# A four-layer transformer in one kernel: set-up order, first mask layout, routing in parts and block indices changed

## The reference

```python
x = x + L0_xattn(layernorm(x), ctx, mask0)     # 16 heads; mask0 is 4 x 1 x 512 x 77, bool
x = x + L0_ffn(layernorm(x))                   # 8 experts, top 2 by softmax, gelu
x = x + L1_xattn(layernorm(x), ctx, mask1)     # 16 heads; mask1 is 4 x 77, int
x = x + L1_ffn(layernorm(x))                   # sum over 8 gated experts, silu, no routing
x = x + L2_xattn(ctx, layernorm(x), mask2)     # 16 heads; mask2 is 1 x 1 x 512 x 77, bool
x = x + L2_ffn(layernorm(x))                   # 1 shared and 8 routed experts, top 2, silu
x = x + L3_xattn(ctx, layernorm(x))            # 8 heads of 128; keys are x's 512 rows and ctx's 77
x = x + L3_ffn(layernorm(x))                   # 8 gated experts, top 2, silu
```

## Time and profile before

| | us |
|---|---|
| runs | 1589.42, 1583.72, 1591.42 |
| median | 1589.42 |
| profiled execution | 1584.89 |
| its span on the core | 1581.8 |
| PE busy | 1386.6 (88%) |
| VectorE busy | 1028.4 (65%) |
| ScalarE busy | 850.9 (54%) |
| GpSimd busy | 545.0 (34%) |

### The profile page before, as it was taken

One profiled execution on the slowest core, in us unless ns is written; L12 is line 12 of the kernel. 1 busy time (PEld: TensorE's weight loads), 2 busy tenths in 40 slices (PEclk: granted clock), 3 DMA queues, 4 the chain that ended last, 5 costly groups with the idle time before them and its releaser, 6 DMA issues.

```text
span 1581.8 us, 21944 instructions
## 1 busy us (share of the span) xinstructions
PE 1386.6 (88%) x7201; PEld 1099.5 (70%) x7201; DVE 1028.4 (65%) x2075; ACT 850.9 (54%) x1608; POOL 545.0 (34%) x880
## 2 busy tenths in 40 slices
PE   3899798798999999889999997699989989875992
PEld 3565576554888888756678885588878878765992
DVE  4545678755666666845567775577777877655773
...
GB/s 153 33 92 2 61 114 94 41 80 63 193 101 99 113 88 120 103 38 61 45 50 107 54 1 1 118 42 1 1 12 5 1 16 1 36 139 117 382 249 87
DMA packets 67790, 123.13 MB, mean 78 GB/s; under 512 B 10200, under 2 KB 43792, under 8 KB 66399
## 3 DMA queue, kind: packets, MB, share of 16 engines
...
...
## 4 chain that ended last, share of the span: by engine, by line
PE 67%; DVE 12%; POOL 10%; issue 7%; ACT 2%; DMA 2%; ACTq 0%; POOLq 0%; DVEq 0%; SPq 0%
PE psum L2003 11%; PE psum L2005 11%; PE psum L2004 11%; PE psum L2248 5%; PE psum L2388 4%; PE psum L2390 4%; PE psum L2389 4%; PE psum L2483 3%; PE psum L2201 2%; PE psum L2202 2%; POOL y_dram L994 2%; POOL slots_dram L963 2%; DMA shared<-in_mask_dram 1%; PE psum L2028 1%; PE psum L2232 1%
## 5 line engine op out<-in xcount | busy, mean ns | idle before, releaser
L1816 DVE TENSOR_TENSOR hhl<-psum,hhl 128x512 fp32r<-128x512 f32 x336 | 230.2, 686 | 83.6 <-ACT hhl L1282 81.5
L1282 ACT ACTIVATE hhl<-psum 128x512 fp32r<-128x512 f32 x336 | 199.3, 593 | 3.4 <-DVE psum L1812 3.2
L2003 PE MATMUL psum<-xh,wl 128*128 128x512 f32 x464 | 189.2, 408 | 3.2 <-DVE hhl L1816 2.5
L2004 PE MATMUL psum<-xl,wh 128*128 128x512 f32 x464 | 184.7, 398 | 0.0
L2005 PE MATMUL psum<-xh,wh 128*128 128x512 f32 x464 | 184.4, 397 | 0.0
L1062 POOL TENSOR_SCALAR shared<-shared,xstat 128x589 f32<-128x589 f32 x128 | 97.7, 765 | 232.4 <-DVE xstat L1906 231.9
L1272 ACT ACTIVATE psum<-psum 128x512 f32<-128x512 f32 x208 | 120.9, 582 | 71.3 <-PE psum L2005 70.0
L1354 ACT ACTIVATE hhl<-psum 128x512 fp32r<-128x512 f32 (+1 forms) x160 | 95.4, 596 | 116.9 <-PE psum L2483 116.6
L2388 PE MATMUL psum<-hhl,wl 128*128 128x512 f32 x336 | 135.0, 402 | 12.8 <-DVE xn L1836 9.4
L1812 DVE TENSOR_TENSOR psum<-act_out,psum 128x512 f32<-128x512 f32 x128 | 89.0, 696 | 84.0 <-PE psum L2005 78.5
L1911 DVE TENSOR_TENSOR hhl<-psum,hhl 128x512 fp32r<-128x512 f32 (+1 forms) x160 | 110.3, 689 | 49.6 <-ACT hhl L1354 49.0
...
## 6 DMA issues: line engine op xcount, KB each, us to landing
...
```

The costliest lines, as they stand in the source:

```text
L1282: a.activation(hh[k % 4], h_bank(f, k), ACT.Copy).then_inc(f.hh_done, 1)
L1816: v.tensor_tensor(hl[k % 4], h_bank(f, k), hh[k % 4].bitcast(f32), ALU.subtract).then_inc(f.h_ready, 1)
L2003: mm(dst, ll, rh, start=start, stop=False)
L2004: mm(dst, lh, rl, start=False, stop=False)
```

## The change

It has six parts.

1. SyncE loads the first batch's x ahead of all else, with a semaphore of its own (`first_loaded`); ScalarE loads the other three batches. VectorE makes the first statistics on that semaphore.
2. The masks of layers 0 and 2 are loaded with four consecutive tokens to a partition (308 bytes in one piece), and `copy_mask` writes them in an order that undoes this. The tiles of masks 1 and 2 lie elsewhere in `shared`.
3. `keys_values(2)`, `first_stats(3)`, `masks` and `gates_split` leave VectorE's set-up for slots 1, 3, 11 and 14 of the first attention, and ScalarE's `keys_high(2)` for slot 0; the column products go from slot 13 to slot 17. The gates are counted on `mask_done`.
4. `rank_routes` is cut in `logits_in`, `compare_routes` and `order_routes`. In the attentions and feed-forward loops the last of them moves one slot later, to the weighing. In the wide loop `logits_in` and `place_rows` move one slot earlier, ahead of the low half of the turned tile, `order_routes` one later, and ScalarE's exponent one later.
5. `mask_keys` of the next layer comes once behind each of the first four splits in the loop instead of four times ahead of them.
6. `block_meta` makes the index with one operation from a destination that already has the offset in it; `valid`, `away` and what is needed for them go from `block_tables`, and rows past an expert's count carry no offset and so fall out of range by themselves.

```diff
-                    13: ("cols", 0), 15: ("x", 3)}, LEFT, LEFT]
+                    17: ("cols", 0), 15: ("x", 3)}, LEFT, LEFT]
...
         def _(sp):
+            sp.dma_start(x[:, tiles(0), :], x_in[0].rearrange("(t p) d -> p t d", p=P)).then_inc(first_loaded, 16)
             sp.dma_start(ctxT[:], ctx_t).then_inc(ctx_loaded, 16)
...
-            sp.dma_start(m2u, mask2.rearrange("b o (t p) k -> p (b o t) k", p=P)).then_inc(late_loaded, 16)
+            sp.dma_start(m2u, mask2.rearrange("b o (p t) k -> p (b o t) k", p=P)).then_inc(late_loaded, 16)
...
-                    sp.wait_ge(tables, 2)
-                at = sp.value_load(tab[0:1, 1, j - NSTAT:j - NSTAT + 1], min_val=0, max_val=NE * CAP - BK)
+                    sp.wait_ge(tables, 1)
+                at = sp.value_load(tab[0:1, 1, j - NSTAT:j - NSTAT + 1], min_val=0, max_val=NE * CAP)
...
                 pool.wait_ge(row_in[j % len(row_in)], row_landed(j))
-                w = wid[j % 4]
+                w, fields = wid[j % 4], rowin[j % RIN][:, :, D:RW].rearrange("p c (w e) -> p c w e", w=2)
                 if j < NSTAT:
-                    fields = rowin[j % RIN][:, :, D:RW].rearrange("p c (w e) -> p c w e", w=2)
-                    if j == 0:
-                        pool.wait_ge(tables, 1)
                     st.link(g.tensor_copy(w, fields[:, :, :, j]))
                 else:
                     if j == NSTAT:
-                        pool.wait_ge(tables, 2)
-                    fields = rowin[j % RIN][:, :, D:RW].rearrange("p c (w e) -> p c w e", w=2)
+                        pool.wait_ge(tables, 1)
                     st.link(g.tensor_tensor(picked, fields, bcast(bcast(dyn[:, j - NSTAT, :], 2, 1), 2, 1), ALU.mult))
                     for n in (4, 2):
                         st.link(g.tensor_tensor(picked[:, :, :, 0:n], picked[:, :, :, 0:n], picked[:, :, :, n:2 * n],
                                                 ALU.add))
                     st.link(g.tensor_tensor(w, picked[:, :, :, 0], picked[:, :, :, 1], ALU.add))
-                st.link(g.tensor_tensor(idf, w[:, :, 1], valid[:, j, :], ALU.mult))
-                st.link(g.tensor_tensor(idf, idf, away[:, j, :], ALU.add))
                 if j >= 4:
                     pool.wait_ge(y_sent[(j - 4) % 3], results_sent((j - 4) // 3 + 1))
-                g.tensor_copy(idx[j % 4], idf).then_inc(meta_ready, 1)
+                g.tensor_scalar(idx[j % 4], w[:, :, 1], FAR, 0.0, ALU.add, ALU.add).then_inc(meta_ready, 1)
...
                     pool.wait_ge(k3_in[l + 1], 16 * 12)
                     pool.wait_ge(t_ready, UL * (l + 1))
-                    for b in range(B):
-                        mask_keys(l + 1, b)
                 for e in range(f.U, f.E):
                     split(f, e)
+                    if l < 2 and e - f.U < B:
+                        mask_keys(l + 1, e - f.U)
                     if f is F1:
...
-                a.activation(maskT[:, mask_slot(l, b), :], src[0:KC, :], ACT.Copy).then_inc(mask_in, 1)
+                a.activation(maskT[:, mask_slot(l, b), :].rearrange("k (p t) -> k t p", t=TB),
+                             src[0:KC, :].rearrange("k (t p) -> k t p", t=TB), ACT.Copy).then_inc(mask_in, 1)
...
-            a.dma_start(x[:], x_in.rearrange("b (t p) d -> p (b t) d", p=P)).then_inc(x_loaded, 16)
-            a.dma_start(m0u, mask0.rearrange("b o (t p) k -> p (b o t) k", p=P)).then_inc(mask_loaded, 16)
+            a.dma_start(x[:, TB:NT, :], x_in[1:B].rearrange("b (t p) d -> p (b t) d", p=P)).then_inc(x_loaded, 16)
+            a.dma_start(m0u.rearrange("p (b t) k -> p b (t k)", b=B),
+                        mask0.rearrange("b o (p t) k -> p (b o) (t k)", p=P)).then_inc(mask_loaded, 16)
...
-            keys_high(2)
...
                     elif u == 0 and l == 0:
-                        act.wait_ge(mask_done, 2)
+                        act.wait_ge(mask_done, 1)
...
+                    if l == 0 and n == 0:
+                        keys_high(2)
...
                             x_turned(b)
-                    for what, b in WPLAN.get(n - 2, []):
+                    for what, b in WPLAN.get(n - 3, []):
                         if what == "l":
                             route_exp(F3, b)
...
-            def rank_routes(f, b, src):
+            def logits_in(f, b, src):
...
-                order_routes(f, b)
-
-            def order_routes(f, b):
+
+            def compare_routes(f, b):
...
                 st.link(v.tensor_tensor(tied, other, mine, ALU.is_equal))
                 st.link(v.tensor_tensor(tied, tied, bcast(tri[:], TB, 1), ALU.mult))
+
+            def order_routes(f, b):
+                c = tiles(b)
+                lg = logits[:, c, :]
+                mine, other = bcast(lg, NE, 3), bcast(lg, NE, 2)
                 st.link(v.tensor_tensor(above, other, mine, ALU.is_gt))
                 st.link(v.tensor_tensor(above, above, tied, ALU.add))
...
-                st.link(v.tensor_copy(rem[:, 0:NSTAT], cnt))
-
-                def validity(j):
-                    n = j.stop - j.start
-                    st.link(v.tensor_tensor(valid[:, j, :], bcast(cols2, n, 1), bcast(rem[:, j], 2, 2), ALU.is_lt))
-                    return v.tensor_scalar(away[:, j, :], valid[:, j, :], -FAR, FAR, ALU.mult, ALU.add)
-
-                validity(slice(0, NSTAT)).then_inc(tables, 1)
...
-                st.link(v.tensor_tensor(pick, dyn, bcast(cnt, NDYN, 1), ALU.mult))
-                st.link(v.tensor_reduce(blk_n, pick, AX.X, ALU.add))
-                st.link(v.tensor_tensor(rem[:, NSTAT:NBLK], blk_n, blk_i, ALU.subtract))
                 st.link(v.tensor_tensor(blk_r, blk_r, blk_i, ALU.add))
                 st.link(v.tensor_scalar(tab[:, 0, :], blk_e, float(NE - 1), None, ALU.min))
-                st.link(v.tensor_scalar(tab[:, 1, :], blk_r, float(NE * CAP - BK), None, ALU.min))
-                validity(slice(NSTAT, NBLK)).then_inc(tables, 1)
+                v.tensor_scalar(tab[:, 1, :], blk_r, float(NE * CAP), None, ALU.min).then_inc(tables, 1)
...
-                v.tensor_scalar(betaB[:], betaB[:], pcols[:, 5:6], None, ALU.mult).then_inc(gate_done, 1)
+                v.tensor_scalar(betaB[:], betaB[:], pcols[:, 5:6], None, ALU.mult).then_inc(mask_done, 1)
...
+            dve.wait_ge(first_loaded, 16)
+            first_stats(0)
             dve.wait_ge(x_loaded, 16)
-            first_stats(0)
...
-            keys_values(2)
-            masks()
-            first_stats(2)
-            first_stats(3)
-            gates_split()
             wide_weights_low(0, 0, bank(3))
             wide_weights_low(0, 1, bank(7))
+            first_stats(2)
+
+            def beside_scores(n):
+                if n == 1:
+                    keys_values(2)
+                elif n == 3:
+                    first_stats(3)
+                elif n == 11:
+                    masks()
+                elif n == 14:
+                    gates_split()
...
+                    if l == 0:
+                        beside_scores(n)
...
-                            rank_routes(f, b, bank(6))
+                            logits_in(f, b, bank(6))
+                            compare_routes(f, b)
...
+                            order_routes(f, b)
...
+                    for what, b in WPLAN.get(n, []):
+                        if what == "l":
+                            logits_in(F3, b, bank(7))
+                        elif what == "c":
+                            place_rows(b)
                     if n >= TURN:
                         turned_low(n - TURN)
                     for what, b in WPLAN.get(n - 1, []):
                         if what == "l":
-                            rank_routes(F3, b, bank(7))
-                        elif what == "c":
-                            place_rows(b)
+                            compare_routes(F3, b)
+                    for what, b in WPLAN.get(n - 2, []):
+                        if what == "l":
+                            order_routes(F3, b)
...
-                pe.wait_ge(gate_done, 1)
+                pe.wait_ge(mask_done, 3)
```

30 lines of the change are left out of this document (14 added, 16 removed).

## The result

| | before | after |
|---|---|---|
| median of 7 runs, us | 1584.76 | 1569.22 |
| lowest to highest | 1583.58 to 1591.42 | 1566.58 to 1576.07 |
| profiled execution: span, us | 1581.8 | 1565.0 |

The ratio is 0.9906, 95% interval 0.9883 to 0.9930: 15.5 us less, where 22.9 were forecast. The changed kernel is faster by more than 0.5%, and its time lies in the stated range.

What follows compares the result with a forecast made beforehand. TensorE work or waits were taken to bound the first attention, with 39.4 us touchable overall. Terms -14.7 + 4.8 + 5.8 - 4.5 - 1.3 - 9.5 - 3.5 = -22.9 gave 1562.0 profiled, 1566.5 us median; range 1553 to 1580.

Steps and rivals of the forecast that it cites:

- Set-up: Before the first score: mask used 7.3 us earlier and a second stall gone, 14.7 us off, 43.0 to 28.3.
- The second stall: Set-up, behind the mask: PE's 6.28 us wait for the score weights' low half goes, with some 1.1 us more: 7.4.
- Rival 3: Set-up: the mask doesn't land earlier, as copies ahead fill the copy engines; the first 7.3 us stay, 1573.8 us; chance 0.11.
- Given back in the slots: First attention: moved VectorE work between score maxima costs +1.8 (slots 1 and 3), +1.2 (slot 11), +1.8 (slot 14), sum +4.8 us.
- The added wait: First attention, batch 2's query tiles: PE waits for query copies behind the later column products, +4.5 and +1.3, sum +5.8 us.
- First feed-forward stage: First expert stage: routing no longer slowed by key masks, PE's 7.69 us stall falls to 3.9; with clock, -4.5 us.
- rival 4: First expert stage: weight splits replace the key masks beside the routing, so the 3.8 us stay, 1570.3 us; chance 0.06.
- Third stage: Third expert stage: the same cut of the routing takes -1.3 us of PE's 1.54 us idle time.
- Wide attention: Wide attention: PE's 11.4 us of waits for logits and row positions go, less a price; -9.5 us (-5 to -11.4).
- The price of 0.6 us a batch: Wide attention: the turned tile's low half comes later, of which PE may feel 0.6 us for each batch.
- rival 2: Wide attention: PE waits for the turned tile's low half instead; 3 of 9.5 us stay, 1573 us; chance 0.14.
- Blocks: Dynamic blocks: GpSimd's period falls from 4.88 to 4.34 us and keeps up; the last weighing starts 3.5 us earlier.

Runs made afterwards that it cites:

- Slot 13: The changed kernel with the column products back in slot 13 of the first attention and the gates in slot 12 instead of 14: 1565.57 us median, ratio 0.9858.

## Why the prediction was right, and where it was too large

The direction and the path of the first attention came as forecast. That the median, 1569.2, is so near to 1566.5 is partly luck: the gain was 15.5 us where 22.9 were forecast, and the level from which I took them off, 1589.4 from three runs, lay 4.7 above the 1584.8 of seven. One part failed by the prediction's own sign, which was over 5 us of stalls kept in the wide stage under another name: 7.5 were kept. Its other sign, a first attention that ends less than 1 or more than 12 us earlier, wasn't met (3.2).

**Set-up: the size was right, the reason half.** First score at 29.3 where 28.3 was forecast, first mask in use at 14.3 where 14.9 was. The second stall went as said: from the first mask operation to the first score it is 15.0 us instead of 20.8, 5.8 less where 7.4 were forecast. That the size of the pieces brings the mask forward was the wrong step: with the old pieces and all else changed it lands after 13.7 us, and with the old x load too after 14.2. Rival 3 asked whether 308 bytes are still dear. The Trainium skill ("DMA: Bandwidth & Descriptors", "Specifications") wants 512 bytes or more for a piece. The traces have 8.7 to 9.6 us for 512 pieces of 308 in five kernels with this set-up against 13.7 for 2048 of 77, so larger pieces help below that size too, but with both the mask was there when VectorE came to it. Not foreseen: x ahead of the weights delays PE's first matmul from 5.75 to 9.56. With x in one load it is at 5.78, and the first score is no earlier (30.2).

**Given back in the slots:** +3.0 for +4.8, but not where I put it. Keys and statistics in slots 1 and 3 cost 2.7 at slot 4, because they stand ahead of the second batch's query half, and that is a longer queue than the gaps between maxima which I counted. Masks and gates cost less than forecast: the gates took 1.4 us in slot 14 (VectorE in order of time, from 71.29 to the end of the last one at 72.67) and not 2.9. In the set-up GpSimd was at work beside them; that this is the reason was not tried apart.

```profile
71.29 0.22 DVE L1615 TENSOR_SCALAR gwg<-gw,pcols 128x8 f32<-128x8 f32 x1
...
72.38 0.29 DVE L1621 TENSOR_SCALAR late<-late,pcols 128x128 f32<-128x128 f32 x1
```


**The added wait:** +6.1 for +5.8, with a stall of 3.63 ended by the query copies and the second tile 4.2 us behind the first. Slot 13 took it away. (In its working the second tile's part, 3.7 less 2.5, is 1.2 and not 1.3.) It is the largest part of what the first attention gives back, and some of it is the lower clock behind the stall, which the prediction didn't count.

**First feed-forward stage:** -4.3 for -4.5; the stall 3.90, forecast 3.9. The key masks alone do it. VectorE's and GpSimd's work there, in order of time:

```profile
183.80 0.19 DVE L1495 TENSOR_TENSOR logits<-logits,rstd 128x32 f32<-128x32 f32 x1
...
184.58 0.42 DVE L1506 TENSOR_TENSOR ctxT<-logits 128x256 bf16<-128x256 f32 x1
```

```profile
197.00 0.63 POOL L940 TENSOR_SCALAR wh<-late 128x512 fp32r<-128x512 f32 x1 [17.91 <-PE psum L2395]
```

The first routing operation takes 0.19 us instead of 1.25 and the last 0.42 instead of 1.50, with nothing of GpSimd's beside them. That is what the sentence of the Trainium skill ("SBUF — State Buffer", "Who interferes with whom") on mutual exclusion would have. GpSimd stood for 17.91 us waiting for PE, so rival 4 had no splits to offer. Later 1.6 us of it were lost again, at a granted clock of 1.00: in four steps between 227 and 247 us PE loses 0.3 to 0.4 us each, the one with a bracket ahead of the product with a hidden tile's low half (246.62, 0.17 us <-DVE hhl). The set-up parts alone lose as much there and the key masks alone nothing, so it goes with the set-up parts; how isn't known.

**Third stage:** 0 for -1.3. I took a bracket for a gain without asking what comes next on that engine. The weighing has to end before PE turns the weights, and the cut leaves its end where it was.

**Wide attention, the step that failed:** -8.1 for -9.5, but by the waits only -3.9. Both waits that I had read went. In their place PE waits for the low half of the weight product, 9.1 us where the kernel before had 1.6 us of waits of that name. The price of 0.6 us a batch for work of VectorE that now comes later was the wrong term; the new waits make 2.5 a batch. It is rival 2 in another form: I had looked at the turned tile's low half and not at that one. The table by stretches, the same stage of before and of the changed kernel (columns as in the table above):

```profile
1140.00:1420.00 280.00, 248.49 (x1513) 217.87 (x1512) 200.44 (x421) 160.73 (x338) 102.06 (x141) 0.97 0.08 30
```

```profile
1134.00:1406.00 272.00, 244.38 (x1514) 215.06 (x1512) 198.91 (x421) 160.07 (x338) 101.73 (x140) 0.98 0.08 31
```

PE's idle time fell from 31.5 to 27.6 us, by 3.9, where 9.5 were forecast. The other 4.1 us are its busy time, with the same matmuls at a higher granted clock, and these are the execution's and not the change's. All fourteen traces show it, over the same 1511 matmuls of the stage (from 1140.03 to 1419.50 in the kernel before; busy time and clock by the table by stretches):

| wide loop | executions | length, us | PE busy, us | PEclk |
|---|---|---|---|---|
| old | 2 | 277.9 | 246.3 | 0.97 |
| old | 3 | 279.5 to 279.8 | 248.0 to 249.1 | 0.96 to 0.97 |
| new | 4, the changed kernel's among them | 271.4 to 271.5 | 243.8 to 243.9 | 0.98 |
| new | 2 | 274.8 | 248.1 to 248.2 | 0.96 |
| new | 3, the wide loop alone among them | 276.5 | 250.9 to 251.0 | 0.95 |

Every execution of the new loop is shorter than every one of the old. The means are 273.9 and 278.9 us, 5.0 less, of which 4.7 are idle time and 0.3 busy time. The timed runs of the wide loop alone say the same, 0.30% or 4.7 us. So the term was worth 5 us, half of the 9.5, and the changed kernel's profiled execution had 3 more by chance.

**Blocks:** -3.0 for -3.5, by the mechanism as forecast: GpSimd's own work of 4.3 us a block lies under the others' pace of 4.7, and it waits for ScalarE. (The block table loses eight operations of VectorE by the diff and not nine; nothing was counted for them.)

**The sum** of the spans' difference was 22.9 and is 16.8, 6.1 us less. By the table, the forecast was too favourable by 0.9 at the first score, 0.3 at the second tile, 1.5 at the end of the first attention, 0.2 in the first feed-forward stage, 1.6 behind it (1.5 and 1.6 are small losses that I had set to nothing), 1.3 in the third stage, 1.4 in the wide attention (5.6 by the waits alone) and 0.5 at the end; it was 1.8 too unfavourable between the slots. These make 5.9; 0.2 more went between the last scatter and the end. In the medians 1569.2 stands for 1566.5: the changed kernel's median lies only 4.2 us above its span where I had 7.6, namely 3.1 around the span and 4.5 from three runs of before, whose median was 1584.8 in seven.
